# Attention layers on one core: a PSUM bank for V and the feed-forward, one bank for the flipped probabilities, two buffers of shifted tokens, and the clip moved onto the sum of squares

## The reference, cut to what matters

```
x = x + ssd_block(layernorm(x))        # state space block, chunks of 64
x = x + layers(layernorm(x))           # two attention layers        <- the change
x = x + scan_block(layernorm(x))       # recurrence over 256 steps, 16 states
x = x + layers(layernorm(x))           # the same two layers again   <- the change
```

```
h = shift_token(x)                     # second half of the features comes from the token before
q, k, v = split(h @ wqkv, 3)           # 512 columns each
q, k = l2norm(q)*qs, l2norm(k)*ks      # l2norm(t) = t / clip(norm(t), 1e-12), per head
q, k = rotary_xpos(q, k)               # two products with tables and a sum
o = local_attention(q, k, v)           # each window of 64 sees itself and the window before
x = x + o @ wo
h = layernorm(shift_token(x))*lg + lb
a, g = split(h @ w1 + b1, 2)           # 341 each
x = x + (a * gelu(g)) @ w2 + b2
```

## Time and profile before

| what | value |
|---|---|
| median of three runs | 2897.46 us (2897.29 to 2911.29) |
| profiled execution: device time | 2903.22 us |
| its span, first to last instruction | 2901.3 us |
| mean granted TensorE clock | 0.936 |
| busy: PE, DVE, ACT, POOL | 2358.4, 1983.2, 1950.0, 1471.6 us |
| layers, first time | from about 366 to 1255 us |
| layers, second time | from about 2010 to 2901 us |

### The profile page before, as it was taken

One profiled execution on the slowest core, in us unless ns is written; L12 is line 12 of the kernel. 1 busy time (PEld: TensorE's weight loads), 2 busy tenths in 40 slices (PEclk: granted clock), 3 DMA queues, 4 the chain that ended last, 5 costly groups with the idle time before them and its releaser, 6 DMA issues. The chain is left out here.

```text
span 2901.3 us, 47111 instructions
## 1 busy us (share of the span) xinstructions
PE 2358.4 (81%) x13516; PEld 1233.4 (43%) x13516; DVE 1983.2 (68%) x5318; ACT 1950.0 (67%) x4833; POOL 1471.6 (51%) x1308
## 2 busy tenths in 40 slices
PE   6999778888888888766766767776888888888887
PEld 3555445545555455422222222222454445544543
DVE  2333367767767677458988989897776676767664
ACT  3444357777777777567877677775777777776674
POOL 1222145545545555347776777774654554554442
PEclk9999879999999999978988888879999999999999
DMA  3000000000000000000000000000000000000000
GB/s 126 1 0 0 1 12 12 12 8 11 12 9 16 8 11 11 4 0 0 1 1 1 0 1 0 1 0 4 12 12 9 12 12 8 16 12 19 15 11 15
DMA packets 12195, 30.41 MB, mean 10 GB/s; under 512 B 2240, under 2 KB 2240, under 8 KB 11456
## 3 DMA queue, kind: packets, MB, share of 16 engines
q1 hardware_dynamic: 11968, 27.99, 3.5%
HBM read 9.11 MB, written 2.10 MB: 4 GB/s over the span
## 5 line engine op out<-in xcount | busy, mean ns | idle before, releaser
L500 POOL TENSOR_TENSOR arena<-arena 128x512 f32<-128x512 f32 x256 | 325.1, 1270 | 782.9 <-DVE arena L1469 782.9
L544 POOL TENSOR_TENSOR arena<-arena 128x512 f32<-128x512 f32 x256 | 328.8, 1301 | 128.5 <-ACT arena L1243 120.4
L1111 ACT ACTIVATE arena<-psum 128x512 f32<-128x512 f32 x256 | 152.6, 596 | 300.9 <-PE psum L824 300.5
L1475 DVE TENSOR_REDUCE SS<-arena 128x8 f32<-128x512 f32 x256 | 174.8, 683 | 259.3 <-ACT arena L1111 257.9
L824 PE MATMUL psum<-rest,HA 128*128 128x512 f32 x512 | 276.5, 623 | 51.1 <-DVE arena L1469 51.1
L513 POOL TENSOR_TENSOR P<-P,RS 128x512 f32<-128x512 f32 x256 | 266.5, 1041 | 93.8 <-DVE RS L1401 92.6
L1555 DVE TENSOR_TENSOR_SCAN arena<-arena,psum 128x512 f32<-128x512 f32 x256 | 310.9, 1215 | 3.2
L910 PE MATMUL psum<-BS,tabs 96*128 96x512 bf16 x384 | 146.7, 443 | 204.2 <-DVE arena L1555 202.4
L979 PE MATMUL psum<-arena,first 128*128 128x512 f32 x512 | 289.7, 655 | 10.9 <-POOL arena L535 10.6
L775 PE MATMUL psum<-HN,rest 128*128 128x512 f32 (+1 forms) x384 | 214.9, 674 | 98.9 <-ACT arena L1126 51.4
L506 POOL TENSOR_TENSOR arena<-arena,SC 128x512 f32<-128x512 f32 x256 | 273.1, 1067 | 29.8 <-DVE SC L1480 29.6
(11 more groups left out here) (222 smaller groups left out, 5878.9 us busy)
## 6 DMA issues: line engine op xcount, KB each, us to landing
arena<-arena SPq DMA_DIRECT2D x128, 128.0 KB, 2.3
rest<-in_rest SPq DMA_DIRECT2D x1, 4183.0 KB, 23.0
X<-in_x SPq DMA_DIRECT2D x1, 2048.0 KB, 11.0
out<-X SPq DMA_DIRECT2D x8, 256.0 KB, 2.4
first<-in_first SPq DMA_DIRECT2D x1, 1445.5 KB, 6.6
tabs<-in_tabs SPq DMA_DIRECT2D x1, 1216.0 KB, 13.5
```

The source lines that it names most:

```text
L500: nc.gpsimd.tensor_tensor(CQ[:, n % 2, :], CQ[:, n % 2, :], SQN[:, n % 2, :], ALU.add).then_inc(f_rope, 1)
L544: nc.gpsimd.tensor_tensor(WU[:, k % DEEP, :], RG[:, k % DEEP, :], U[t.j % 2][:, k % 2, :], ALU.mult).then_inc(m_wu, 1)
```

## The change

Four things change, all in the `layers` blocks.

1. PSUM: the flipped probabilities use bank 2 alone; `flip` of step g therefore waits until the flipped probabilities of g-1 have been copied out (`f_pta` g instead of g-1). Bank 3 becomes `V_BANK`, used by the V projection and by every other feed-forward matmul. Bank 6 is left to `to_features` alone, whose only bank wait is now its own previous copy.
2. Shifted tokens: `HA` becomes two buffers. `begin_slot` at place 0 is replaced by `shift_ahead` at place 10, which fills the buffer for piece j+2 during slot j. Its waits are on things of earlier slots and on the outer layernorm of pair j+2, made at place 7 of the same slot.
3. Clip: instead of bounding the inverse norm from above on DVE (`clipped` at place 6+4n, tile SC), DVE bounds the sum of squares from below (tile SM to SS), between the first and the second product. ACT's Ln then has no bias, and POOL's `scaled` waits for ACT's Exp directly.
4. The second hardware loop covers slots 9 to 12 (two turns); 13 and 14 are written out.

```diff
-        HA = sb("HA", [128, NT])
+        HA = [sb(f"HA{k}", [128, NT]) for k in range(2)]
...
-        S_BANK, P_BANK, O_BANK = (bank[0], bank[1]), (bank[2], bank[3]), bank[4]
-        QK_BANK, T_BANK = bank[5], bank[6]
-        HID_BANK = ((T_BANK, STAT, T_BANK), (STAT, T_BANK, STAT))
+        S_BANK, P_BANK, O_BANK = (bank[0], bank[1]), bank[2], bank[4]
+        QK_BANK, T_BANK, V_BANK = bank[5], bank[6], bank[3]
+        HID_BANK = ((V_BANK, STAT, V_BANK), (STAT, V_BANK, STAT))
...
+                self.ahead = last + 2 < SLOTS
...
-            with eng.Fori(0, PAIRS // 2 - 1) as i:
+            with eng.Fori(0, PAIRS // 2 - 2) as i:
                 for j in (PAIRS + 1, PAIRS + 2):
-                    slot(Slot(eng, ph, i, j, j + PAIRS - 4))
-            for n in (SLOTS - 1, SLOTS):
+                    slot(Slot(eng, ph, i, j, j + PAIRS - 6))
+            for n in range(SLOTS - 3, SLOTS + 1):
                 slot(Slot(eng, ph, 0, n))
...
             def scaled(k, m, n):
                 k.wait_ge(f_rope, 8, n + 1, slot=m)
-                k.wait_ge(f_sc, 8, n + 1, slot=m)
+                k.wait_ge(f_sr, 8, n + 1, slot=m)
...
             def flip(k, m, g):
                 k.wait_ge(f_rp, 8, g + 1, slot=m)
-                k.wait_ge(f_pta, 8, g - 1, slot=m)
+                k.wait_ge(f_pta, 8, g, slot=m)
...
                 elif k.pre:
-                    k.wait_ge(f_qkt, 8, 3, slot=1)
+                    k.wait_ge(f_v, 4, 3, slot=1)
                 elif k.has(0):
-                    k.wait_ge(f_qkt, 8, 8)
+                    k.wait_ge(f_v, 4, 4)
                 hidden(k, 1, m, f_g)
 
             def other_half(k, m):
                 if m == 0:
-                    if k.pre:
-                        k.wait_ge(f_qkt, 8, 4, slot=1)
                     k.wait_ge(f_ge, 3, 2, slot=-1)
...
             def project_v(k, tt):
                 k.wait_ge(f_h, 1, 1, slot=1)
-                if tt < 2:
-                    if k.has(0):
-                        k.wait_ge(f_qkt, 8, 7 + tt)
-                    elif tt == 1:
-                        k.wait_ge(f_v, 4, 1, slot=1)
-                else:
-                    k.wait_ge(f_qkt, 8, 4 * tt - 6, slot=1)
+                if tt == 3 and k.post:
+                    k.wait_ge(f_ga, 3, 3, slot=-1)
+                elif tt:
+                    k.wait_ge(f_v, 4, tt, slot=1)
+                elif k.has(0):
+                    k.wait_ge(f_v, 4, 4)
...
             def to_features(k, m, n):
                 part = n % 2
                 k.wait_ge(f_qk, 8, n + 1, slot=m)
-                if n in (1, 5):
-                    k.wait_ge(f_qkt, 8, n, slot=m)
-                elif n == 6:
-                    k.wait_ge(f_v, 4, 4, slot=m)
...
+                k.wait_ge(f_qkt, 8, n, slot=m)
...
-            def begin_slot(k):
-                if k.layer(1):
-                    k.wait_ge(f_r2, 1, 1, slot=1 - PAIRS)
+            def shift_ahead(k):
+                if k.layer(2):
+                    k.wait_ge(f_r2, 1, 1, slot=2 - PAIRS)
                 else:
-                    k.wait_pair(outer.out, 1)
+                    k.wait_pair(outer.out, 2)
                 k.wait_ge(f_pj, 8, 8)
                 k.wait_ge(f_vp, 4, 4)
-                shifted(R[:, k.tokens(1)], HA, f_h)
+                shifted(R[:, k.tokens(2)], HA[k.side(2)], f_h)
...
             def clipped(k, m, n):
-                k.wait_ge(f_sr, 8, n + 1, slot=m)
-                k.wait_ge(f_qk, 8, n - 1, slot=m)
-                TS(SC[:, n % 2, :], SR[:, n % 2, :], NORM_CLIP, None, ALU.min).then_inc(f_sc, 1)
+                k.wait_ge(f_sm, 8, n + 1, slot=m)
+                TS(SS[:, n % 2, :], SM[:, n % 2, :], SS_CLIP, None, ALU.max).then_inc(f_ss, 1)
...
-                if k.pre and h == 0:
-                    begin_slot(k)
+                if k.ahead and h == 10:
+                    shift_ahead(k)
```

More of the change, by code:

```diff
@@ L31 @@
 SS_SCALE = 2.0 ** 32
-SS_FLOOR = 2.0 ** -63
 LN_UNSCALE = 16 * float(np.log(2.0))
-NORM_CLIP = 1e12
+SS_CLIP = 1e-24
 EPS = 1e-5
@@ L130, in program @@
         eps_col = sb("eps_col", [128, 1])
-        floor_col = sb("floor_col", [128, 1])
         unscale_col = sb("unscale_col", [128, 1])
@@ L210, in program @@
         SR = sb("SR", [128, 2, HEADS])
-        SC = sb("SC", [128, 2, HEADS])
+        SM = sb("SM", [128, 2, HEADS])
         NB = sb("NB", [128, 2, 2, 2])
@@ L248, in program @@
         f_sr = sem("f_sr")
-        f_sc = sem("f_sc")
+        f_sm = sem("f_sm")
         f_prod = sem("f_prod")
@@ L732, in flip @@
                         at = 256 * r + 128 * tile
-                        last = nc.tensor.transpose(P_BANK[g % 2][:, at:at + 128],
+                        last = nc.tensor.transpose(P_BANK[:, at:at + 128],
                                                    P[:, 2 * (g % 2) + r, 128 * tile:128 * tile + 128], F("ident"))
@@ L823, in project @@
                 k.wait_ge(f_prod, 8, n, slot=m)
-                mm(QK_BANK, HA[:, 128 * tt:128 * tt + 128],
+                mm(QK_BANK, HA[k.side(m)][:, 128 * tt:128 * tt + 128],
                    W(f"wqkv{k.layer(m)}", INNER * part, INNER * part + INNER), start=True, stop=True).then_inc(f_pj, 1)
@@ L841, in to_features @@
                 k.wait_ge(f_qk, 8, n + 1, slot=m)
-                if n in (1, 5):
-                    k.wait_ge(f_qkt, 8, n, slot=m)
-                elif n == 6:
-                    k.wait_ge(f_v, 4, 4, slot=m)
-                elif n == 7:
-                    if k.pre:
-                        k.wait_ge(f_v, 4, 1, slot=m + 1)
-                    else:
-                        k.wait_ge(f_qkt, 8, n, slot=m)
-                elif n in (0, 2):
-                    k.wait_ge(f_v, 4, 2 + n // 2, slot=m)
-                elif k.post:
-                    k.wait_ge(*((f_ge, 3, 2) if n == 3 else (f_ga, 3, 3)), slot=-1)
-                else:
-                    k.wait_ge(f_qkt, 8, n, slot=m)
+                k.wait_ge(f_qkt, 8, n, slot=m)
                 for c in range(4):
@@ L1088, in flipped @@
                 k.wait_ge(f_ptp, 8, g + 1, slot=m)
-                A(PT[:, g % 2, :], P_BANK[g % 2], ACT.Copy).then_inc(f_pta, 1)
+                A(PT[:, g % 2, :], P_BANK, ACT.Copy).then_inc(f_pta, 1)
             def square_centred(norm, wait, centred, square):
@@ L1114, in values @@
                 k.wait_ge(f_vp, 4, tt + 1, slot=1)
-                A(VT[k.side(1)][:, tt, :], T_BANK, ACT.Copy).then_inc(f_v, 1)
+                A(VT[k.side(1)][:, tt, :], V_BANK, ACT.Copy).then_inc(f_v, 1)
             def norms(k, m, n):
                 k.wait_ge(f_ss, 8, n + 1, slot=m)
-                A(SL[:, n % 2, :], SS[:, n % 2, :], ACT.Ln, bias=floor_col[:, :], scale=SS_SCALE).then_inc(f_sl, 1)
+                A(SL[:, n % 2, :], SS[:, n % 2, :], ACT.Ln, scale=SS_SCALE).then_inc(f_sl, 1)
                 k.wait_ge(f_sl, 8, n + 1, slot=m)
@@ L1270, in _ @@
             v.memset(eps_col[:, :], EPS)
-            v.memset(floor_col[:, :], SS_FLOOR)
             v.memset(unscale_col[:, :], LN_UNSCALE)
             v.memset(XN[:, :, 0:CONV - 1], 0.0)
-            v.memset(HA[:, :], 0.0)
+            v.memset(HA[0][:, :], 0.0)
+            v.memset(HA[1][:, :], 0.0)
             v.memset(HF[:, :], 0.0)
@@ L1459, in products @@
                 k.wait_ge(f_sq, 8, n + 1, slot=m)
-                k.wait_ge(f_ss, 8, n + 1, slot=m)
                 k.wait_ge(f_xp, 8, n - 1, slot=m)
@@ L1465, in products @@
                    t[:, part, :].unsqueeze(1).to_broadcast([128, HEADS, DH]), ALU.mult)
+                clipped(k, m, n)
                 y = SQN[:, part, :].rearrange("p (h r d) -> p h r d", h=HEADS, r=2)
@@ L1516, in dve_dense @@
                     products(k, *item(k, h, 2))
-                if item(k, h, 4):
-                    clipped(k, *item(k, h, 4))
             def dve_slot(k):
```

6 lines of the change are left out of this document (3 added, 3 removed).

## The result

| | before | changed |
|---|---|---|
| median, both measured side by side | 2898.41 us (2897.29 to 2911.29, 4 runs) | 2794.38 us (2791.43 to 2801.32, 4 runs) |
| ratio, 95% interval | | 0.9635 [0.9602, 0.9667] |
| profiled execution | 2903.22 us | 2801.32 us |
| its span, mean granted clock | 2901.3 us, 0.936 | 2799.5 us, 0.941 |
| busy: PE, DVE, ACT, POOL | 2358.4, 1983.2, 1950.0, 1471.6 us | 2320.1, 1919.9, 1925.3, 1472.8 us |

The changed kernel is 104 us faster.

The account below looks back on a forecast made before the run. PE was busiest, 44.8 of 51.2 us a slot, with waits of 6.4. Border 51.6, feed-forward 5.6, loops 3.8 and clock 5 sum to 66 us: 2903.2 to 2837.2 profiled, median 2832; forecast 2810 to 2850 (72%), range with rivals 2808 to 2864.

Parts of the forecast that it names:

- The bank at the border: Slot border: the V projection no longer waits for ACT's copy of item 5's transposes; 0.89 us gained.
- fourth rival: The change does not do what it says: bank 6's wait returns on bank 3; only the loops gain, 2893 us; 3%.
- The shift at the border: Slot border: sums follow ACT's squares without the shift between; 0.9 us gained, some 0.5 us of PE's wait staying.
- The feed-forward: Second feed-forward half: gate product slightly earlier, 0.2 us a slot, 5.6 in all; the other 1.6 us become another wait.
- The clip: Clip moved to the sum of squares on DVE: 256 instructions of 0.20 us median change place; nothing gained.
- The shift at place 10: Shift at its new place: costs nothing; at the other end 0.4 us a slot, 12 us in all.
- The loops: Second hardware loop: one back edge and two looped slots fewer in each block run; 3.8 us gained.
- The clock: Clock falls at the feed-forward, 13 costing some 19.4 us: a quarter, 5 us, counted as gained.
- The filling: Edges of the block runs: not in the sum; "something at the edges" only in the forecast's low end, 2810 us.
- Only the bank pays: Rival: something besides the shift holds the slot border, so only 0.89 us a border remains; 2867 us; 12%.
- One fall in each slot: Rival: feed-forward waits bring a clock fall in each of 30 slots, 45 us lost; 2863 us; 10%.
- falls at both gaps and at the border: Rival: three clock falls in each slot, 4.5 us a slot, 135 in all; slower, 2953 us; 3%.

Follow-up runs that it names:

- no_clip: The changed kernel with the clip on the inverse norm again and Ln with its floor as bias; 2807.64 us.
- self_wait: The changed kernel with DVE's products waiting for the end of the sums once more; 2810.05 us.
- bank_only: The kernel before with the PSUM part alone: one flip bank, bank 3 for the V projections and every other feed-forward matmul; 2873.32 us.
- loop_only: The kernel before with slots 13 and 14 written out and nothing else; 2903.06 us.
- after_again: The changed kernel once more, unedited, as yardstick; 2792.34 us.
- gate_table: The changed kernel with DVE's gate products at places 20 and 22, and ACT's table load for exponentials behind item 4's squares; 2793.26 us.
- gap_back: The changed kernel with a needless wait: the second feed-forward half's first matmul waits for ACT's copy of item 3's transposes; 2822.82 us.
- no_shift: The changed kernel with one buffer of shifted tokens, filled at the slot border again; 2842.65 us.
- no_bank: The changed kernel with the bank taken back: V, feed-forward and transposes share one bank, two flip banks; 2852.45 us.
- shift_only: The kernel before with shifted tokens in two buffers, filled at place 10 of the slot before, and slots 13 and 14 written out; 2861.61 us.
- clip_only: The kernel before with the clip alone moved to the sum of squares, Ln without a bias; 2892.11 us.

## Why the prediction was wrong

It had the direction and the place right. Three terms of its sum failed: the clock, of whose falls a quarter was counted as gained (5 us) where nearly all went (18 us); the filling of the pipeline, which the sum put at nothing and which gave 14.9; and the clip on DVE's chain at the feed-forward, counted as a loss of 0.14 us where the chain got shorter. The shift at the border was sized a little low too. Its sum of 66 us against the 101.8 us between the two spans:

| term | predicted | profiled |
|---|---|---|
| slots at full clock (border 51.6, feed-forward 5.6, loops 3.8) | 61 | 72.8 |
| clock falls inside the slots | 5 | 18.0 |
| filling of the pipeline, twice | 0 | 14.9 |
| between the block runs, and the two ends | 0 | -3.8 |
| sum | 66 | 101.8 |

The first line is the sum, over the slots of a block run, of the length before and after with 1.5 us taken off for each fall; the second is the rest of the 90.8 us, for 14 falls before and 2 after. The fourteenth lies in the short last window of the first block run; the prediction's 13 of 30 windows had missed it. The terms are rounded. The sign that I had named for the slots, 49.1 to 49.4 us, fell with the sum: they last 48.4.

**The bank at the border**, 0.89 us: 1.05. The wait went as said, and the wait on bank 3 that the fourth rival feared didn't come. I had let the V projection start at the end of the transposes as recorded, 0.60 us behind their start; it starts 0.44 behind it, before 1.49 (815.38 to 816.87 in the earlier trace rows).

**The shift at the border**, 0.9: 1.07 (4.99 to 3.92 us between the two `project`), with the clip inside. I had worked out 4.1 us from `project` to `project`; with the old clip it is 3.96 in no_clip, with the new one 3.92, so the clip inside, which I had counted with 0.14 us, costs nothing, because the first product no longer waits for the sums' end. I had also left 0.5 us of PE's wait standing. Of it 0.11 is left, for another reason besides: the transposes ahead of that `project` start 0.23 us later behind the one before (787.21 to 790.36, before 817.80 to 820.72), when POOL's scaling of their item is done (789.26 + 1.04).

**The feed-forward**, 0.2 us a slot: 0.6. I gave DVE's gate product 0.29 us for PE's wait, less 0.14 for the clip. In the trace it starts 20.72 us behind the inner mean, before 21.31 (804.81 - 783.50), 0.59 earlier: 0.29 from PE's wait, 0.10 because ACT reaches the squares earlier, and 0.2 because DVE's chain of sums and products got shorter with the clip in it. That third part is the step that failed here: the clip ran free of POOL's operation and took 0.16 us behind a product, and the wait between the sums and the first product went. The runs split the 0.6 us at the next `project`: with the bank alone it starts 0.42 us earlier behind the inner mean (22.61 us, before 23.03), and the clip's move is the other 0.2 (22.42, in no_clip 22.62). With the wait of self_wait put back it starts at 22.60; the `project` of the border then comes 0.12 us later still, 0.3 us a slot at the two places. The other 1.57 us did change from one wait into the other, as said.

**The clip** was counted at nothing. It gave 6.7 us alone and 9 in company (104.0 - 95.3), medians that agree with 0.2 us in each of 30 slots but could not show it by themselves. Beside DVE's chain, ACT's Ln takes 0.21 us without its bias, where it took 0.30 (medians of 256); its share was not measured by itself.

**The shift at place 10** cost nothing, as said. Its second half was blocked by POOL (median 1.17 us); its first, which started before POOL's operation (755.75 and 755.91), was not (0.39). The Trainium skill's rule (SBUF — State Buffer, "Who interferes with whom") foretells the blocking, and the trace agrees; my reading of it as two blocked halves, 2.9 us, was too dear at this place (1.57 us, 755.75 to 757.32). Two blocked halves stand at the border of bank_only (1.25 and 1.17 us, 2.4 together), where I had not looked for them.

**The loops** were a misreading. I took the looped slots as 0.5 us longer than the written-out ones. The row of the longer slot has one DVE instruction more (133, not 132), and it is this one, which the last of the layers has in every slot, looped or not:

```profile
919.61 0.69 DVE L1446 TENSOR_TENSOR X<-X,arena  x1
```

In loop_only the window of slot 13, now written out, lasts 51.7 us in both block runs, as it did in the loop. What was left, the back edge, is 0.9 us (52.6 against 51.7), once less in each block run, and the medians can't tell that from nothing. In the changed kernel the slot with the back edge takes 50.8 us without a fall (after_again and gate_table, one block run each) where its neighbours take 48.9, so there it costs 1.9.

**The clock** was the step with the largest error for its size: 5 us said, 18 measured. I took a quarter of the falls as gained, because the gaps only moved and one grew. Of 13 falls in the 28 full slots 2 are left, both at a back edge. In the trace before, nine of the 13 begin at the end of the wait of 1.83 us in front of `other_half`; the other four are at the border, behind waits of 1.58, 1.72 and 2.84 us (the last a double fall), where in a plain slot it is 1.48. The wait of 1.4 us at the gelu stood in every slot and had none behind it. Such a list over all slots would have told me to take out the nine with their wait, and to ask only whether the new wait of 1.57 us brings its own: it brings none in 28 slots. The experiments show it for the feed-forward: bank_only has none there, and gap_back has 12 again with its wait of 1.8 to 1.9 us. For the border they show less. no_shift has four of its eight falls behind a border wait of 1.77 us, but the length of one wait isn't all of it: the two falls of the changed kernel stand behind waits of 1.62 and 1.34 us beside a back edge, and five of bank_only's stand behind waits of 0.6 us and less. Why falls come at the border of some slots and not of others stays open.

**The filling** was left out of the sum; I had put it into the low end of the range as "something at the edges". Windows from the copy of the first piece to the first inner mean, both block runs before, and then after:

```profile
357.70:463.44 105.74, 85.44 (x521) 45.54 (x522) 68.77 (x227) 66.07 (x198) 51.47 (x46) 0.82 0.05 12
2007.07:2108.57 101.50, 79.64 (x521) 42.81 (x521) 69.10 (x227) 64.63 (x197) 51.64 (x46) 0.90 0.05 12
```

```profile
358.06:454.27 96.21, 80.90 (x521) 43.78 (x521) 65.07 (x228) 64.21 (x198) 51.54 (x46) 0.85 0.06 13
1959.27:2055.42 96.15, 80.81 (x521) 43.69 (x522) 65.36 (x228) 62.95 (x197) 51.72 (x46) 0.85 0.06 13
```

The clock doesn't explain the gain: the second filling is 5.4 us shorter at a lower mean clock, 0.85 in place of 0.90. The clock does move it by some microseconds, though: before, the two fillings take 105.7 us at 0.82 and 101.5 at 0.90. The other profiled kernels point at the bank first. Without it the two fillings take 102.6 and 101.9 us (no_bank), without the shift 99.0 and 97.2, without the clip 100.4 and 97.2; with the bank alone 100.8 and 98.3, with the shift alone 106.5 and 105.2. Each is one execution, so only the bank's share is clear, and what in it makes the filling shorter was not looked into; it stays open.

**The rivals.** "Only the bank pays" fell: the shift alone gave 37 us. "One fall in each slot" and "falls at both gaps and at the border" fell with 2 falls in 28 slots; the mechanism is real, though: falls come at the border in bank_only, and at the feed-forward in gap_back. "The change does not do what it says" fell.

## What to carry to other kernels

Two changes that clear the same short stretch of one engine's queue are not to be summed: work out each with the other in place, since the first brings the second's work forward into whatever runs beside it. Before pricing the clock, list PE's waits over all slots and mark which of them a fall follows; if the change takes that wait out, take out its falls, and look for a wait that grows to its length elsewhere, and for several short ones that come in a row. Compare the slots first, and the medians second: a part that no edit touched varied by 17 us here. And when two windows differ, look first at the counts of instructions in their rows.

## What the runs showed of the hardware that I had not expected

- The clock: the same wait of 1.82 to 1.91 us in front of the second feed-forward half was followed by a fall to half speed for 3.4 us in 9 of 28 slots before, in 6 in shift_only and loop_only, 8 in clip_only, 13 in no_bank and 12 in gap_back; a wait of 1.57 us two matmuls later in none. Each such fall costs 1.5 us. At the border of bank_only, falls also came behind three waits of 0.4 to 0.6 us in a row, in five of six such slots (in no_shift, in one of eight).
- A DVE instruction that needn't wait for the one ahead starts about 0.1 us before that one's end: the first product follows the start of the sums by 0.60 us (788.90 to 789.50), where the reduction takes 0.69. With a wait for its end in between the first product follows by 0.78 us (self_wait), and the slot grew by 0.3 us at two places.
- ACT's Ln on 8 columns takes 0.30 us with a bias from SBUF and 0.21 without.
